# Routing tokens to expert tiles in a two-layer kernel: rows kept in token order and gathered, instead of scattered to slots; two of the router's logit groups moved

## The reference, cut to what matters

```python
logits = jnp.einsum('th,eh->te', x, router_w)          # 2048 tokens, 8 experts
top_vals, top_idx = jax.lax.top_k(logits, TOP_K)       # TOP_K = 2
top_w = jax.nn.softmax(top_vals, axis=-1)
expert = top_idx[:, 0]
weight = top_w[:, 0]
gate = jnp.einsum('th,eih->eti', x, gate_w)
up = jnp.einsum('th,eih->eti', x, up_w)
act = jax.nn.silu(gate) * up
out_e = jnp.einsum('eti,ehi->eth', act, down_w)
combine = jax.nn.one_hot(expert, e, dtype=x.dtype) * weight[:, None]
out = jnp.einsum('eth,te->th', out_e, combine)
```

## Time and profile before

| | us |
|---|---|
| median of 3 runs | 2169.09 |
| lowest, highest | 2164.94, 2176.32 |
| the profiled execution | 2165.28 |
| its span | 2163.6 |
| attention of layer 0, its last part (1139.6 to 1164.3) | 24.7 |
| routing (1164.3 to 1200.4) | 36.1 |
| experts (1200.4 to 1406.4) | 206.0 |
| layer 1 (1406.4 to 2163.6) | 757.2 |

### The profile page before, as it was taken

One profiled execution on the slowest core, in us unless ns is written; L12 is line 12 of the kernel. 1 busy time (PEld: TensorE's weight loads), 2 busy tenths in 40 slices (PEclk: granted clock), 3 DMA queues, 4 the chain that ended last, 5 costly groups with the idle time before them and its releaser, 6 DMA issues. The chain is left out here.

```text
span 2163.6 us, 40241 instructions
## 1 busy us (share of the span) xinstructions
PE 1910.5 (88%) x14497; PEld 1188.2 (55%) x14497; DVE 1599.1 (74%) x3508; ACT 1363.0 (63%) x3321; POOL 1111.4 (51%) x868
## 2 busy tenths in 40 slices
PE   0789999999999999999986699967898889878999
PEld 0456566666666666666656455535666565633444
DVE  7799988888878887888852499757778686834760
ACT  6587777677677677777753244246867686835442
POOL 5677776686676676566632366444323132200540
PEclk9999999999999999999996899969999999889999
DMA  4434432322223212343215744375424243335100
GB/s 177 129 113 135 125 110 74 112 70 91 76 82 96 86 60 95 129 138 119 80 40 204 311 143 146 115 263 164 149 91 155 75 150 120 118 128 194 39 20 19
DMA packets 110978, 256.46 MB, mean 119 GB/s; under 512 B 10945, under 2 KB 39745, under 8 KB 108737
## 3 DMA queue, kind: packets, MB, share of 16 engines
q1 hardware_dynamic: 91520, 204.65, 28.5%
q10 hardware_dynamic: 16704, 40.90, 5.4%
q0 software_dynamic: 2560, 8.39, 1.1%
HBM read 175.52 MB, written 75.24 MB: 116 GB/s over the span
## 5 line engine op out<-in xcount | busy, mean ns | idle before, releaser
L1009 PE MATMUL ps_q<-a_y,a_w 128*128 128x512 f16 x1536 | 344.3, 381 | 57.7 <-POOL a_y L704 57.6
L1009 PEld LDWEIGHTS ps_q<-a_y,a_w 128*128 128x128 f16 x1536 | 148.1, 98 | 225.8 <-issue 61.0
L727 POOL TENSOR_TENSOR a_rb<-a_rb,router_y 128x512 f32<-128x512 f32 x128 | 181.0, 1414 | 167.0 <-ACT a_rb L870 166.2
L1220 DVE TENSOR_REDUCE a_nmax<-ps_s 128x1 f32<-128x512 f32 (+3 forms) x256 | 123.6, 483 | 103.4 <-PE ps_s L1030 103.1
L869 ACT ACTIVATE a_rb<-ps_q 64x512 f32<-64x512 f32 x128 | 76.1, 594 | 169.9 <-DVE a_ra L1205 168.3
L1018 PE MATMUL ps_v<-a_w,a_y 128*128 128x128 f16 x3072 | 182.0, 219 | 0.0
L1056 PE MATMUL ps_o<-a_tt_,a_v 128*128 128x512 f32 (+3 forms) x512 | 156.0, 448 | 22.4 <-ACT a_tt_ L912 18.9
L1018 PEld LDWEIGHTS ps_v<-a_w,a_y 128*128 128x128 f16 x3072 | 174.3, 98 | 1.2
L1078 PE MATMUL ps_v<-a_o,a_wo 128*128 128x512 f16 x732 | 169.6, 382 | 1.9 <-ACT a_v L896 1.9
L889 ACT ACTIVATE ps_s<-ps_s,a_nmax 128x512 f32<-128x512 f32 (+3 forms) x256 | 125.3, 489 | 40.3 <-DVE a_nmax L1222 40.2
L2175 ACT ACTIVATE a_ef<-ps,a_nmax 128x512 f32<-128x512 f32 (+3 forms) x256 | 131.9, 537 | 22.7 <-DVE a_nmax L2539 21.1
(11 more groups left out here) (333 smaller groups left out, 4977.1 us busy)
## 6 DMA issues: line engine op xcount, KB each, us to landing
a_w<-wqkv_split SPq DMA_DIRECT2D x48, 768.0 KB, 4.6
scratch_numlog<-wkv_nl ACTq DMA_DIRECT2D x40, 512.0 KB, 2.7
wkv_kt<-in_fT ACTq DMA_DIRECT2D x56, 256.0 KB, 2.9
router_y<-in_wqkv SPq DMA_DIRECT2D x16, 768.0 KB, 5.4
wqkv_split<-a_w SPq DMA_DIRECT2D x16, 768.0 KB, 6.9
a_stacks<-qk_parts SPq DMA_DIRECT2D x96, 128.0 KB, 2.6
gate_up<-in_gate_up SPq DMA_DIRECT2D x8, 1408.0 KB, 11.1
a_nlc<-scratch_numlog SPq DMA_DIRECT2D x17, 512.0 KB, 4.6
```

The costliest lines, as they stand in the source:

```text
L727: pool.tensor_tensor(rb[:, n, :], rb[:, n, :], rot[:, 2 * n + 1, :], ALU.mult).then_inc(s["roped"], 1)
L1009: mm = pe.matmul(psq[n][:], w16[:, g % 2, wp, n, c, :], y16[b % 2][:, yp, c, :], start=c + m == 0, stop=c == CC - 1 and m == 2)
L1220: dve.tensor_reduce(nmax[:, 0, j:j + 1], cols(ps, j), AX, ALU.max, negate=True)
```

## The change

The rows no longer go to slots. ACT stores each batch's rows in token order to `token_x` (four plain DMAs of 1 MB), and SP waits for them at the block's end. Which token sits in which slot is computed: for each group of 128 tokens DVE makes a one-hot table of the lane (slot modulo 128, `on_lane`) and one of the tile, multiplied by the token's number (`on_tile`); 16 float16 products on PE, summed in PSUM, give `row_of`: for every lane and tile the token's row (0 where a slot is empty). In the experts' block POOL gathers each tile by `row_of` with one indirect DMA, 23 in all, ahead of its scan work in every iteration. POOL's instructions in that block are issued in the same iterations as DVE's, where they had been issued unit by unit.

Only 2 experts' weights are loaded in the routing block; SP loads the other 6 at the start of the experts' block, and then counts the experts that have arrived (`experts`), which POOL did before. The first 6 result tiles are stored by ACT, the others by SP. The load and transposition of a 24th tile, which nobody used, are gone, as are the zeros of `slot_x`. In the routing block DVE and PE no longer wait for all of POOL's constants, the prefix sums come ahead of the softmax weights, and only two row groups are turned before the prefix sums.

In the attention block, the logits of batch 0 are computed in slot 64 and those of batch 1 in slot 65, ahead of `turn`.

```diff
@@ -1110,6 +1097,10 @@
                         pe.wait_ge(s["swapped"], HEADS * 2)
                         pe.wait_ge(s["o_lo"], HEADS - 1)
                         output_heads(OUTPUTS - 4, 0, G - 1)
+                    if p >= HEADS:
+                        pe.wait_ge(s["router"], 16)
+                        pe.wait_ge(s["swapped"], HEADS * 2)
+                        logits(p - HEADS)
                     if p >= 2:
                         turn(p - 2)
                         values(p - 2)
...
@@ -1120,8 +1111,7 @@
                     output_heads(n, G - 1, G)
                 pe.wait_ge(s["acc"], OUTPUTS - 4)
                 output_heads(OUTPUTS - 1, 0, G)
-                pe.wait_ge(s["router"], 16)
-                for b in range(B):
+                for b in range(LAST - HEADS, B):
                     logits(b)
 
...
-EARLY = 4
+EARLY = 2
...
+        late_spare = w.down[:, E - 2].rearrange("p k c -> p (k c)")
+        on_lane = late_spare[:, 0:NT * P // 2].bitcast(F16).rearrange("p (t n) -> p t n", n=P)
+        on_tile = late_spare[:, NT * P // 2:NT * (P + SLOT_TILES + 1) // 2].bitcast(F16).rearrange(
+            "p (t n) -> p t n", n=SLOT_TILES + 1)[:, :, 0:SLOT_TILES]
+        last_spare = w.down[:, E - 3].rearrange("p k c -> p (k c)")
+        at_least = last_spare[:, 0:NT * (SLOT_TILES + 1)].rearrange("p (t n) -> p t n", t=NT)
+        in_tile = last_spare[:, 512:512 + NT * SLOT_TILES].rearrange("p (t n) -> p t n", t=NT)
...
 
             @block.sync
             def _(sp):
                 for e in range(EARLY):
                     w.load(sp, e)
+                sp.wait_ge(s["kept"], 16 * B)
 
             @block.gpsimd
...
-                pool.wait_ge(s["slots"], 1)
-                for i in range(NT):
-                    pool.wait_ge(s["rows"], i + 1)
-                    pool.indirect_dma_start(d["slot_x"], bass.IndirectOffsetOnAxis(ap=k.slot[:, i:i + 1], axis=0),
-                                            rows[:, i, :], None).then_inc(s["scattered"], 16)
-                pool.wait_ge(s["scattered"], 16 * NT)
...
+                    act.wait_ge(s["rows"], b * TT + TT)
+                    act.dma_start(d["token_x"][b * T:(b + 1) * T].rearrange("(t p) c -> p t c", p=P),
+                                  rows[:, b * TT:(b + 1) * TT, :]).then_inc(s["kept"], 16)
...
                 turn_rows(0)
+                turn_rows(1)
                 pe.wait_ge(s["math"], 2)
-                pe.wait_ge(s["const"], 8)
+                pe.wait_ge(s["const"], 6)
                 pe.matmul(pss[:, 0:NT * E], prior[:], chosen.rearrange("p e t -> p (e t)"), start=True, stop=False)
                 pe.matmul(pss[:, 0:NT * E], ones[:], upto.rearrange("p e t -> p (e t)"),
                           start=False, stop=True)
                 pe.matmul(pss[:, NT * E:NT * E + E], ones[:], upto[:, :, NT - 1], start=True,
                           stop=True).then_inc(s["sums"], 1)
-                for b in range(1, B):
-                    turn_rows(b)
+                for i in range(2, NT):
+                    turn_rows(i)
+                pe.wait_ge(s["on_tile"], 1)
+                for i in range(NT):
+                    if i % TT == 0:
+                        pe.wait_ge(s["on_lane"], i // TT + 1)
+                    mm = pe.matmul(pss[:, 256:256 + SLOT_TILES], on_lane[:, i, :], on_tile[:, i, :],
+                                   start=i == 0, stop=i == NT - 1)
+                mm.then_inc(s["tokens"], 1)
...
-                dve.tensor_copy(k.slot[:], slotf[:]).then_inc(s["slots"], 1)
+
+                then(dve.tensor_tensor(at_least, wide(slotf[:], SLOT_TILES + 1),
+                                       tile_start[:].unsqueeze(1).to_broadcast([P, NT, SLOT_TILES + 1]), ALU.is_ge))
+                then(dve.tensor_reduce(begun[:], at_least, AX, ALU.add))
+                then(dve.scalar_tensor_tensor(out=lane_of[:], in0=begun[:], scalar=-float(P), in1=slotf[:],
+                                              op0=ALU.mult, op1=ALU.add))
+                then(dve.tensor_tensor(in_tile, at_least[:, :, 0:SLOT_TILES], at_least[:, :, 1:], ALU.subtract))
+                dve.tensor_tensor(on_tile, in_tile, wide(token[:], SLOT_TILES), ALU.mult).then_inc(s["on_tile"], 1)
+                for b in range(B):
+                    tt = slice(b * TT, (b + 1) * TT)
+                    dve.tensor_tensor(on_lane[:, tt, :], wide(lane_of[:, tt], P),
+                                      lane[:].unsqueeze(1).to_broadcast([P, TT, P]), ALU.is_equal).then_inc(s["on_lane"], 1)
 
                 then(dve.tensor_tensor(past, tile_no[:], ends[:].unsqueeze(1).to_broadcast([P, SLOT_TILES, E]),
                                        ALU.is_ge))
                 then(dve.tensor_reduce(expertf[:], past, AX, ALU.add))
                 then(dve.tensor_scalar(expertf[:], expertf[:], float(E - 1), None, ALU.min))
                 then(dve.tensor_copy(k.tile_expert[:], expertf[:]))
+                then(dve.tensor_copy(k.slot[:], slotf[:]))
+                dve.wait_ge(s["exp"], 1)
+                then(dve.tensor_scalar(diff[:], diff[:], 1.0, None, ALU.add))
+                then(dve.reciprocal(k.weight[:], diff[:]))
+                dve.wait_ge(s["tokens"], 1)
+                then(dve.tensor_copy(k.row_of[:], pss[:, 256:256 + SLOT_TILES]))
 
 
 def moe_experts(k, w, w1):
...
@@ -1559,53 +1590,54 @@
         def unit(u):
             return u // CC, u % CC * LAYERS + LAYER
 
+        def store(eng, j):
+            eng.wait_ge(s["y"], j + 1)
+            eng.dma_start(d["slot_y"][j * P:(j + 1) * P, :], yo[:, j % 2, :]).then_inc(s[f"stored{j % 2}"], 16)
+
         with nc.Block() as block:
 
             @block.sync
             def _(sp):
+                for e in range(EARLY, E):
+                    w.load(sp, e)
+                for e in range(E):
+                    sp.wait_ge(w.loaded[e], 32)
+                    sp.sem_inc(s["experts"], 1)
+                for j in range(ACT_STORES, SLOT_TILES):
+                    store(sp, j)
+                for i in range(2):
+                    sp.wait_ge(s[f"stored{i}"], 16 * ((SLOT_TILES + 1 - i) // 2))
+
+            @block.gpsimd
+            def _(pool):
+
                 def load(j):
                     if j >= 2:
-                        sp.wait_ge(s["x_ps"], j - 1)
-                    sp.dma_start(xin[:, j % 2, :], d["slot_x"][j * P:(j + 1) * P, :]).then_inc(s[f"x{j % 2}"], 16)
-
-                def store(j):
-                    sp.wait_ge(s["y"], j + 1)
-                    sp.dma_start(d["slot_y"][j * P:(j + 1) * P, :], yo[:, j % 2, :]).then_inc(s[f"stored{j % 2}"], 16)
+                        pool.wait_ge(s["x_ps"], j - 1)
+                    pool.indirect_dma_start(xin[:, j % 2, :], None, d["token_x"],
+                                            bass.IndirectOffsetOnAxis(ap=k.row_of[:, j:j + 1], axis=0)
+                                            ).then_inc(s[f"x{j % 2}"], 16)
+
+                def sums(i):
+                    u, step = divmod(i, 4)
+                    if step == 1:
+                        wkv.pool_eukv(pool, u % 2, u)
+                    if step == 2 and u + 1 < UNITS:
+                        wkv.pool_ekv(pool, (u + 1) % 2, u + 1)
+                    if step == 3:
+                        wkv.join(pool, u, u % 2, u // 2)
+                        if u % 2 and u // 2 < EARLY_PIECES:
+                            w1.pool_low(pool, raw, u // 2)
 
                 load(0)
                 load(1)
-                for e in range(EARLY, E - 2):
-                    w.load(sp, e)
-                for j in range(SLOT_TILES):
-                    if j + 2 <= SLOT_TILES:
+                wkv.pool_ekv(pool, 0, 0)
+                load(2)
+                for j in range(1, SLOT_TILES):
+                    if j + 2 < SLOT_TILES:
                         load(j + 2)
-                    if j < 2:
-                        w.load(sp, E - 2 + j)
-                    store(j)
-                for i in range(2):
-                    sp.wait_ge(s[f"stored{i}"], 16 * ((SLOT_TILES + 1 - i) // 2))
-
-            @block.gpsimd
-            def _(pool):
-
-                def ready(e):
-                    pool.wait_ge(w.loaded[e], 32)
-                    pool.sem_inc(s["experts"], 1)
-
-                for e in range(EARLY):
-                    ready(e)
-                wkv.pool_ekv(pool, 0, 0)
-                for e in range(EARLY, E - 2):
-                    ready(e)
-                for u in range(UNITS):
-                    wkv.pool_eukv(pool, u % 2, u)
-                    if u + 1 < UNITS:
-                        wkv.pool_ekv(pool, (u + 1) % 2, u + 1)
-                    wkv.join(pool, u, u % 2, u // 2)
-                    if u < 2:
-                        ready(E - 2 + u)
-                    if u % 2 and u // 2 < EARLY_PIECES:
-                        w1.pool_low(pool, raw, u // 2)
+                    for i in scans(j):
+                        sums(i)
 
```

(37 more changed lines are left out.)

54 lines of the change are left out of this document (22 added, 32 removed).

## The result

The changed kernel takes 2152.3 us (median of 4 runs) against 2169.7 for the kernel before; the ratio is 0.9917, 95% interval 0.9895 to 0.9939. Repeated with 6 runs of the changed kernel beside 11 of the kernel before it was 0.9917 again, 0.9903 to 0.9932. That is 17 us less; the prediction was 2147 us, 22 less.

The account below looks back on a forecast made before the run. Limits differ by block: PE in the attention drain and experts, DMA bytes and POOL's scatters in routing. Terms -6 - 11 - 2 = -19 to -20 on 2165.3 gave 2145.5; the middle of both bases gave 2147 us, range 2136 to 2164.

Parts of the forecast that it names:

- part 1: Attention block: logits of batches 0 and 1 moved to slots 64 and 65; net -6 us, best -10.6, worst +1.
- part 3: Experts block: first tile +4 us, later tiles -6, unused 24th transposition -0.4; sum -2 us, best -5.
- The size of the shift: Attention block: logits(0) in slot 64 makes the outputs behind it end 5.0 us later.
- best case: Attention block: 3.5 us of shift and values(63) at full clock, giving -10.6 us.
- I take half of that: Attention block: half of the 2.9 us that turn and values lose at half clock, for a shift of 5.0 us.
- Rival (a): Attention block: logits(0) brings PE to 1.2 GHz, the chain moves; +1 us instead of -6, total 2154; chance 0.14.
- Part 2: Routing block: 8.66 MB take 21.5 us, plus 3.6 at head and tail, 25.1 us; -11 us, bounds -16 and -6.
- hidden, unless SP cannot put 12 in the queue at once (+5): Experts block: PE's wait for `experts` behind SP's 12 issues, 5.5 us, ends before the first tile; otherwise +5 us.
- late tiles: Experts block: gathers issued two iterations ahead remove waits for tiles late from DRAM, over 21 iterations; -6 us.
- (b): Experts block: gathers stretch DVE to 8.95 us an iteration; +12 us, total near 2165; chance 0.13 with the page's rule.
- (c): Experts block: each gather holds DVE twice, 10.1 us an iteration; +37 us instead of -6, total 2189; chance 0.06.
- Rival (d): Routing block: the stores land late and the block keeps its length; total 2156 us; chance 0.07.

Follow-up runs that it names:

- logits_last: Changed kernel with all four batches of logits back behind the last output piece; median 2159.8 us, ratio 0.9974 to the kernel before.
- the nine: Nine profiles, the changed kernel twice and seven follow-up kernels, all with both logits batches moved; drains 57.8 to 62.3 us, mean 59.9.
- early4: Changed kernel with four experts' weights loaded in the routing block instead of two; routing block 35.0 us, total 2157.6 us in one run.
- `EARLY = 1` kernels: Changed kernel with one expert's weights in the routing block instead of two, and SP's order altered; routing 19.4 and 18.9 us in two of them.
- gather_twice: Changed kernel with each gather from tile 3 on issued a second time into an unused tile; total 2171.5 us in one run.
- early1_count: Changed kernel with one expert's weights in the routing block, SP counting loaded experts before issuing the other loads; 2143.0 us in one run.
- early1_gather: Changed kernel with one expert's weights in the routing block, the others issued after the first two gathers land; 2149.4 us, ratio 0.9915.
- logits_65: Changed kernel with only one batch of logits moved, into slot 65, none in slot 64; drain 61.4 us in one profile.

## Why the prediction was right, step by step

The forecast was a sum of 19 to 20 us less; 17 were measured, for reasons that held in parts 1 and 2. That the total came out so near is partly luck: in the profiled execution part 1 gave 4.1 us more than forecast and part 3 5.7 us less, and the two nearly cancel.

*Part 1, -6.* The drains give -7.1 against `logits_last` and -7.9 against the kernel before. The shape was right (shift in slot 64, idle time filled in slot 65, two batches left, the last waiting for `k.yr`), and so were the prices: 3.6 us a batch at the higher clock, 7.0 for the last at the lower. The size of the shift was too large. The logits behind the last output piece start 0.6 to 5.1 us later than before, counted from turn(61), 2.7 in the mean of the nine, where 5.0 was forecast: in four of the nine turn(63) ran at the full clock, which the sum had kept for its best case. The profile's -10 is one of the fortunate executions. "I take half of that", for what logits(0) does to the clock behind it, is what the nine profiles bear out: turn(62) took 2.13 to 2.38 us in all of them, half clock or near it, and values(62) 2.58 to 4.00 against 2.40, half clock for a part. Rival (a) was right that the clock falls under a single batch of logits, where I had counted on its falling only after the 5.4 us read off the tail, and wrong about the price: -7.1, not +1.

*Part 2, -11.* Measured -11.3, and `early4` and the `EARLY = 1` kernels confirm the term itself, bytes over 0.403 MB/us plus 3.6 us: 36 forecast and 35.0 measured, 19.5 and 18.9 to 19.4. Its two halves were each off, in opposite directions: 0.92 x 24.7 = 22.7 us of fully busy engines instead of 21.5, and 2.0 us at head and tail instead of 3.6.

*Part 3, -2.* Measured +3.7. The step that failed is the start. The first tile cost +6.3 us, not +4 (the bound was 8): I put the gather's landing at 7.5 us after the block's start and it was near 10. And "hidden, unless SP cannot put 12 in the queue at once (+5)" was the case: it could not, and the block paid 2.8 us. Of the 9.9 us by which gate_up(1) is late, 6.3 and 2.8 are accounted for so; the last 0.8 have no experiment. The rest held: (8.392 - 8.118) x 21 = 5.7 us for the late tiles (6 forecast), and gate_up(22) to the block's end is 0.44 us shorter without the 24th transposition (0.4 forecast).

*The price of a gather on POOL* was wrong in a way that cost nothing here. I used 0.94 us, from gathers with DVE half idle; the 23 in the experts block took

```profile
L1617 POOL DMA_INDIRECT me_xin<-scratch_token_x,row_of x23: 944/1727/1972, 1179.7 to 1358.0; - x23
```

(minimum, median, maximum in ns). POOL had 1.1 us left, not 1.8. What the time goes to stands in the timeline:

```profile
1244.76 1.45 DVE L295 TENSOR_TENSOR_SCAN wkv_bwd<-wk_decay,wkv_tail,wkv_fwd 128x512 f32<-128x512 f32 x1
1245.27 1.73 POOL L1617 DMA_INDIRECT me_xin<-scratch_token_x,row_of  x1
```

This gather starts with 0.94 us of a scan still to run and ends 0.79 us behind that scan's end. Of the 23 gathers, 16 start while a scan runs; they take 1.72 to 1.97 us and end 0.8 us behind the scan. The other seven, at whose start no scan runs, take 0.94 to 1.18 us. So a gather waits for the scan that it meets, and what it costs depends on where in the scan it starts. The direction of the rule I quoted from the Trainium skill (SBUF — State Buffer, section "SBUF: two separate sides"), that a DMA whose descriptors POOL writes is held up by DVE, agrees; the size of the page's example, five times beside a copy, was not reached: here it was 1.8 times at the median and 2.1 at most, beside scans. Rivals (b) and (c) were refuted by DVE's 7.71 and 7.68 us an iteration, but `gather_twice` shows how near they were: with one more gather per tile DVE is busy for 1.0 us more an iteration, near the 1.13 that I had put on (b).

*Rival (d)* was wrong: the block became 11.3 us shorter. As `early4` shows, that holds only because fewer weights stand beside the stores.

## What to carry to other kernels

Ask of a block that ends in a wait for DMAs what its bytes cost before asking what its instructions cost: here the 16 scatters looked like the bottleneck, and loading two experts later gave nearly all of the gain. Moving the bytes to the next block's start is free only if the first transfer that the next block needs does not stand beside them, and if the engine that issues them has nothing to signal behind its issues. Fill an idle gap with off-path work first: here it returned some 6 us. The same work put where the engine has no gap returned 1.5 us by one profile, which the spread between executions does not let one call certain.

## What the runs showed of the hardware that was not expected

SP issued ten loads of weights at about half a microsecond each; in the changed kernel the 11th took 6.71 us, in `early1_count` the 11th 3.41 and the 13th 8.44, and in `early1_gather` the first twelve went at 0.33 to 0.54 us and the 13th took 8.39. So it is not a fixed number of issues; what is counted, transfers under way or bytes, was not tried.

A gather of 256 KB in rows of 2 KB lands 4 to 5 us after its issue with no weights beside it (ACT's 0.8 MB of loads stand there in every kernel), and about 9 us after it beside the weights' long transfers. One expert's 2.2 MB delay it as much as six experts' 13.4 MB. The Trainium skill says that a DMA engine takes turns between the queues, a whole packet at a time (DMA: Bandwidth & Descriptors, section "Queues, rings and completion order"); a delay that does not grow with what is queued would agree with that, but no run here varied the length of a packet.

TensorE's clock fell to 1.2 GHz with no idle time ahead of it, while PE ran the logits' products of 8 columns (`logits_65`: 1.00 until 1123, 0.50 from 1124 on). Where it fell differed between executions, and the same code drained in anything from 57.8 to 62.3 us.
